# Decoder layer: projections of q, k, v from scaled f16 halves of x, turned by DMA

## The reference

```python
qkv = x @ Wqkv                      # 512 -> 3 x 512
q, k = rmsnorm(q, q_norm_w), rmsnorm(k, k_norm_w)        # over all 512, eps 1e-6
q, k = rope(q), rope(k)             # 16 heads of 32
o = softmax(mask(q k^T / sqrt(32))) v ; x = layernorm(x + o @ Wo)
# cross attention over features: 8 heads of 16 TOKENS each, 512 x 512 scores
qk = einsum('bdm,bdn->bmn', x_heads, ctx_heads) / 4
x = layernorm(x + einsum('bmn,bcn->bcm', softmax(qk), ctx_heads))
# fp8 (e4m3) quantise and dequantise of x and of the weight, blocks of 128
x = layernorm(x + qdq(x) @ qdq(W).T)
```

## Time and profile before

| | us |
|---|---|
| median of 3 runs | 2799.9 (2793.93 to 2802.55) |
| profiled execution, its own time | 2798.56 |
| its span in the trace | 2796.8 |
| TensorE busy | 2586.9 (92%) |
| VectorE busy | 2252.9 (81%) |
| ScalarE busy | 2030.6 (73%) |
| GpSimd busy | 1535.7 (55%) |

### The profile page before, as it was taken

How to read it: one execution, slowest core, us unless ns; L and a number is a source line. 1 busy time by engine, 2 the same in 40 slices (tenths; PEclk the granted TensorE clock), 3 DMA queues, 4 the chain that set the end, 5 groups by cost and what they waited for, 6 DMA issues and landing times.

```text
span 2796.8 us, 65074 instructions
## 1 busy us (share of the span) xinstructions
PE 2586.9 (92%) x19088; PEld 1156.4 (41%) x19088; DVE 2252.9 (81%) x3405; ACT 2030.6 (73%) x2945; POOL 1535.7 (55%) x2393
## 2 busy tenths in 40 slices
PE   0679999999999999999999999999999999999774
PEld 0444444444444444444444444444444444444211
DVE  6247888888888888888888888888888888888751
ACT  0235777887778778887888777877887788777653
POOL 1243556655665556655665566655665566556422
PEclk9779999999999999999999999999999999999866
DMA  2133344434443344434343444334443444344211
GB/s 88 38 82 96 93 115 100 118 96 113 109 111 100 106 118 101 110 97 120 99 117 95 114 106 114 100 105 118 102 109 96 121 99 115 98 115 98 84 37 30
DMA packets 534121, 278.46 MB, mean 100 GB/s; under 512 B 401057, under 2 KB 483105, under 8 KB 534049
## 3 DMA queue, kind: packets, MB, share of 16 engines
q1 hardware_dynamic: 534048, 277.56, 38.4%
HBM read 108.09 MB, written 85.46 MB: 69 GB/s over the span
## 4 chain that ended last, share of the span: by engine, by line
PE 79%; DVE 5%; POOL 5%; ACT 4%; issue 4%; DMA 4%; SPq 0%; ACTq 0%; DVEq 0%; POOLq 0%
PE bank L912 27%; PE pv L1042 15%; PE mx L1015 9%; PE st L1029 9%; PE bank L1051 6%; ACT pp L601 3%; PE bank L979 2%; PE bank L961 2%; DMA xdT<-xd 2%; PE bank L948 2%; PE bank L905 2%; PE bank L951 2%; PE bank L982 2%; DVE nm L761 1%; POOL yq L561 1%
## 5 line engine op out<-in xcount | busy, mean ns | idle before, releaser
L761 DVE TENSOR_REDUCE nm<-mx 128x2 f32<-128x1024 f32 x1024 | 1252.3, 1223 | 265.7 <-PE mx L1015 245.5
L601 ACT ACTIVATE pp<-st,esc 128x1024 f32<-128x1024 f32 x1024 | 1139.7, 1113 | 321.5 <-PE st L1029 259.7
L1042 PE MATMUL pv<-pp,vT 128*32 128x512 f32 x4096 | 550.4, 622 | 0.4 <-ACT pp L601 0.2
L1029 PE MATMUL st<-qp,kp 50*128 50x512 f16 x2048 | 402.8, 390 | 36.2 <-ACT pp L601 34.5
L1015 PE MATMUL mx<-kp,qp 48*128 48x512 f16 x2048 | 401.8, 389 | 28.1 <-DVE nm L761 26.6
L912 PE MATMUL bank<-w_h,xT_h 128*128 128x512 f32 x768 | 349.9, 456 | 4.8 <-DVE xT_l L807 4.7
L912 PE MATMUL bank<-w_l,xT_h 128*128 128x512 f32 x768 | 308.1, 401 | 0.0
L912 PE MATMUL bank<-w_h,xT_l 128*128 128x512 f32 x768 | 305.8, 398 | 0.0
L1015 PEld LDWEIGHTS mx<-kp,qp 48*128 48x128 f16 x2048 | 99.3, 93 | 373.6 <-DVE nm L761 189.9
L912 PEld LDWEIGHTS bank<-w_h,xT_h 128*128 128x128 f32 x768 | 146.6, 191 | 169.8 <-issue 135.7
L528 POOL TENSOR_SCALAR_AFFINE_SELECT p<-p 128x512 f32<-128x512 f32 x256 | 162.9, 636 | 95.1 <-ACT p L644 95.0
(11 more groups left out here) (138 smaller groups left out, 4648.9 us busy)
## 6 DMA issues: line engine op xcount, KB each, us to landing
qp<-q_rows SPq DMA_DIRECT2D x256, 96.0 KB, 2.5
kp<-k_rows SPq DMA_DIRECT2D x256, 96.0 KB, 2.3
xb<-x SPq DMA_DIRECT2D x64, 256.0 KB, 2.6
x_rows<-x SPq DMA_DIRECT2D x64, 256.0 KB, 2.1
q_rows<-qpl SPq DMA_DIRECT2D x64, 256.0 KB, 2.8
cx<-ctx SPq DMA_DIRECT2D x64, 256.0 KB, 2.8
k_rows<-kpl SPq DMA_DIRECT2D x64, 256.0 KB, 2.8
x<-x_rows SPq DMA_DIRECT2D x64, 256.0 KB, 2.8
```

What stands on the lines that cost most here:

```text
L601: a.activation(pp[:, unit % 2, 2 * l:2 * (l + 1), :], st[:], ACT.Exp, scale=esc[b.i][:])\
L761: v.tensor_reduce(cols, mx[:], AX.X, ALU.max, negate=True).then_inc(mx_free, 1)
L1029: last = t.matmul(st[:, q, :], kp[b.i][rows, p, i * P:(i + 1) * P], qp[b.i][rows, p, :], start=True, stop=True)
L1042: last = t.matmul(pv[32 * j:32 * j + 2 * XD, :], vT[b.i][:, i, GROUPS * j + g, :], pp[:, unit % 2, j, :], start=(i == 0), stop=(i == KC - 1))
```

## The change

- Weights `w_h`, `w_l` are f16 halves of Wqkv times a power of two, found in the set-up from the sum of squares. High halves are made by ScalarE, low ones by VectorE; the feed-forward weight takes its scale from its sum of squares too, and the round trip of its maximum through memory is gone. Each quantised block takes its own maximum in the loop over blocks.
- x is no longer transposed by TensorE. ScalarE squares it (`x_square`), TensorE sums over partitions (`x_sum`, two one-column products, the second adds a tiny constant), VectorE makes the scale (`x_exp`), ScalarE and GpSimd the scaled f16 halves (`x_high`, `x_scale`, `x_low`), and SyncE turns them (`turn_x`) into `xsT`. The projections use the helper `split`, which the feed-forward product now uses too.
- q and k keep the scale through the rms (the epsilon is scaled along, `xeps`), v is scaled back when it is copied out (`vinv`).
- `xb` has one buffer; the residual rows are loaded a second time, into `xr` (`ld_xr`).
- `pp` has four units in place of two.
- `ctx_sum` gets the tiny constant too. `junkd` has one buffer per layer norm.
- The five tables of steps and `BANK` are new. The tables of SyncE and TensorE are shown.

```diff
-        w_h, w_l = sb("w_h", [P, KC, 3 * D], F32R), sb("w_l", [P, KC, 3 * D], F32R)
+        w_h, w_l = sb("w_h", [P, KC, 3 * D], F16), sb("w_l", [P, KC, 3 * D], F16)
...
-        xb = [sb(f"xb{i}", [P, D]) for i in range(2)]
-        cx, cxs = sb("cx", [P, D]), sb("cxs", [P, D])
-        xT_h, xT_l = sb("xT_h", [P, D], F32R), sb("xT_l", [P, D], F32R)
+        xb, xr = sb("xb", [P, D]), sb("xr", [P, D])
+        cx, cxs, xf = sb("cx", [P, D]), sb("cxs", [P, D]), sb("xf", [P, D])
+        xs, xsT = sb("xs", [P, 2, D], F16), sb("xsT", [P, 2 * KC, P], F16)
...
+        pp = sb("pp", [P, PB, GH, D])
...
+            ld_kp:1@5 st_qpl:0@4 ld_qp:1@5 turn_xd:0@8 turn_x:0@1 ld_x2r:0@7 ld_qp:0@4 ld_x:0@0
+            st_out:0@8 st_sh1:0@2 st_kpl:0@4 ld_sh1:0@2 ld_kp:0@4 st_sh2:0@5 st_x2:0@3 ld_xr:0@2
+            ld_sh2:0@5 turn_parts:0@1 ld_cx:0@3 turn_parts:1@1""")
...
+            cross_scores_T:10@6 proj_k:2@1 proj_k:3@1 cross_scores:14@5 proj_v:0@1 proj_v:1@1
+            self_scores_T:0@2 cross_scores_T:11@6 cross_scores:15@5 proj_v:2@1 proj_v:3@1
+            self_scores_T:1@2 cross_scores_T:12@6 cross_scores:0@4 cross_pv:3@6 self_pv:0@2
+            self_scores_T:2@2 cross_scores_T:13@6 self_pv:1@2 cross_scores:1@4 self_scores_T:3@2
+            cross_pv:4@6 self_pv:2@2 cross_scores:2@4 cross_scores_T:14@6 self_pv:3@2 cross_pv:5@6
+            cross_scores_T:15@6 cross_scores:3@4 cross_pv:6@6 context_T:0@4 cross_scores_T:0@5
+            x_sum:0@0 cross_pv:7@6 cross_scores:4@4 cross_scores_T:1@5 proj_o:0@2 proj_o:1@2
+            cross_scores:5@4 cross_scores_T:2@5 proj_o:2@2 proj_o:3@2 cross_scores:6@4
+            cross_scores_T:3@5 self_scores:0@1 self_scores:1@1 ctx_sum:0@3 cross_pv:0@5
+            cross_scores:7@4 cross_scores_T:4@5 self_scores:2@1 ffn:0@7 ffn:1@7 cross_scores_T:5@5
+            cross_scores:8@4 ffn:2@7 ffn:3@7 cross_scores_T:6@5 cross_scores:9@4 proj_q:0@0
+            self_scores:3@1 cross_scores_T:7@5 cross_scores:10@4 proj_q:1@0 proj_q:2@0
+            cross_scores_T:8@5 cross_scores:11@4 proj_q:3@0 proj_k:0@0 proj_k:1@0 cross_scores:12@4
+            cross_scores_T:9@5 cross_pv:1@5 cross_pv:2@5 cross_scores:13@4""")
...
             def ld_x(b, _):
-                sp.wait_ge(*freed("wo", b, -2))
-                sp.sem_inc(passed_sp, 1)
-                sp.dma_start(xb[b.i][:], x[b.idx()]).then_inc(d_x[b.i], 16)
+                sp.wait_ge(s_xsl, b.n(1, 0))
+                sp.sem_inc(passed_sp, 1)
+                sp.dma_start(xb[:], x[b.idx()]).then_inc(d_x, 16)
+
+            def ld_xr(b, _):
+                sp.wait_ge(*freed("wo", b, -1))
+                sp.sem_inc(passed_sp, 1)
+                sp.dma_start(xr[:], x[b.idx()]).then_inc(d_xr, 16)
...
+            def turn_x(b, _):
+                sp.wait_ge(s_xsl, b.n(1, 1))
+                sp.sem_inc(passed_sp, 1)
+                sp.wait_ge(*full("v", b, -1))
+                sp.sem_inc(passed_sp, 1)
+                sp.dma_start_transpose(xsT[:], xs[:].rearrange("p a d -> p (a d)")).then_inc(d_xsT, 16)
...
+            def x_scale(b, _):
+                pool.wait_ge(s_sx, b.n(1, 1))
+                pool.sem_inc(passed_pool, 1)
+                g_.tensor_scalar(xf[:], xb[:], sx[b.i][:], 1.0, ALU.mult, ALU.mult).then_inc(s_xf, 1)
+                g_.tensor_scalar(xeps[b.i][:], sx[b.i][:], sx[b.i][:], weps[:], ALU.mult, ALU.mult).then_inc(s_xeps, 1)
+
+            def x_low(b, _):
+                pool.wait_ge(s_xf, b.n(1, 1))
+                pool.sem_inc(passed_pool, 1)
+                pool.wait_ge(s_xsh, b.n(1, 1))
+                g_.tensor_tensor(xs[:, 1, :], xf[:], xs[:, 0, :], ALU.subtract).then_inc(s_xsl, 1)
...
+            for c in range(KC):
+                act.wait_ge(d_setup[c], 16)
+                a.activation((qp[0], qp[1], qs, ks)[c][:].bitcast(BF16).rearrange("p a d -> p (a d)")[:, 0:3 * D],
+                             pp[:, c].rearrange("p a d -> p (a d)")[:, 0:3 * D], ACT.Square,
+                             accum_out=wss[:, 0, c:c + 1]).then_inc(u_wss, 1)
+            act.wait_ge(d_wffn, 16 * KC)
+            for c in range(KC):
+                a.activation((junk, junkc, junkd[0], junkx)[c][:], wf_rows[c][:], ACT.Square, accum_out=wss[:, 1, c:c + 1]).then_inc(u_wss, 1)
+            act.wait_ge(u_wsc, 1)
+            for n in range(2 * KC):
+                hi = (w_h, wo_h)[n // KC]
+                src = pp[:, n % PB].rearrange("p a d -> p (a d)")[:, 0:hi.shape[2]]
+                act.wait_ge(d_setup[n % PB], 16 * (n // PB + 1))
+                a.activation(hi[:, n % KC, :], src, ACT.Copy, scale=(wsc[:, 0:1], 1.0)[n // KC]).then_inc(u_high, 1)
...
-                act.wait_ge(pv_unit, b.n(UNITS, unit - 1))
-                a.activation(pp[:, unit % 2, 2 * l:2 * (l + 1), :], st[:], ACT.Exp, scale=esc[b.i][:])\
+                act.wait_ge(pv_unit, b.n(UNITS, unit + 1 - PB))
+                a.activation(pp[:, unit % PB, 2 * l:2 * (l + 1), :], st[:], ACT.Exp, scale=esc[b.i][:])\
                  .then_inc(st_free, 1)
...
-            def xT_high(b, _):
-                act.wait_ge(*full("v", b, -1))
-                act.wait_ge(*full("xT", b))
-                a.activation(xT_h[:], at("xT")[:], ACT.Copy).then_inc(s_xTh, 1)
+            def x_square(b, _):
+                act.wait_ge(d_x, b.n(16, 16))
+                act.wait_ge(*full("xt", b, -1))
+                act.wait_ge(s_xss, b.n(1, 0))
+                a.activation(junkx[:], xb[:], ACT.Square, accum_out=xss[:]).then_inc(s_xss, 1)
+
+            def x_high(b, _):
+                act.wait_ge(s_sx, b.n(1, 1))
+                act.wait_ge(d_xsT, b.n(16, 0))
+                a.activation(xs[:, 0, :], xb[:], ACT.Copy, scale=sx[b.i][:]).then_inc(s_xsh, 1)
...
-            def xT_low(b, _):
-                dve.wait_ge(s_xTh, b.n(1, 1))
-                v.tensor_tensor(xT_l[:], at("xT")[:], xT_h[:].bitcast(F32), ALU.subtract)\
-                 .then_inc(bank_free[BANK["xT"]], 1)
+            def x_exp(b, _):
+
+                dve.wait_ge(*full("xt", b))
+                v.tensor_scalar(xbits[:], at("xt")[:, 0:1].bitcast(I32), -0.5, SCALE_TOP, ALU.mult, ALU.add)\
+                 .then_inc(bank_free[BANK["xt"]], 1)
+                dve.wait_ge(*freed("xt", b))
+                dve.wait_ge(s_xsl, b.n(1, -1))
+                dve.wait_ge(s_xeps, b.n(1, -1))
+                v.tensor_scalar(sx[b.i][:].bitcast(I32), xbits[:], EXP_BITS, None, ALU.bitwise_and).then_inc(s_sx, 1)
+                dve.wait_ge(s_sx, b.n(1, 1))
+                dve.wait_ge(*freed("v", b, -2))
+                v.tensor_scalar(vinv[b.i][:].bitcast(I32), sx[b.i][:].bitcast(I32), -1.0, wtop[:], ALU.mult, ALU.add)\
+                 .then_inc(s_vinv, 1)
...
+            def split(name, lin, wh, wl, cols, part):
+
+                for i, (lo, w) in enumerate(((0, wh), (0, wl), (1, wh))):
+                    last = t.matmul(at(name)[:], lin[:, KC * lo + part, :], w[:, part, cols], start=(part == 0 and i == 0),
+                                    stop=(part == KC - 1 and i == 2))
+                if part == KC - 1:
+                    last.then_inc(bank_full[BANK[name]], 1)
+
+            def x_sum(b, _):
+                pe.wait_ge(s_xss, b.n(1, 1))
+                pe.wait_ge(*before("xt", b))
+                t.matmul(at("xt")[:, 0:1], ones[:], xss[:], start=True, stop=False)
+                t.matmul(at("xt")[:, 0:1], ones[:], tiny[:], start=False, stop=True).then_inc(bank_full[BANK["xt"]], 1)
 
             def proj_q(b, part):
                 if part == 0:
-                    for point in last_of(
-                            freed("xT", b),
-                            before("q", b),
-                    ):
-                        pe.wait_ge(*point)
-                linear("q", xT_h, xT_l, w_h, w_l, slice(0, D), part)
+                    pe.wait_ge(d_xsT, b.n(16, 16))
+                    pe.wait_ge(*before("q", b))
+                split("q", xsT, w_h, w_l, slice(0, D), part)
...
-                t.matmul(at("ct")[:, 0:1], ones[:], css[:], start=True, stop=True).then_inc(bank_full[BANK["ct"]], 1)
+                t.matmul(at("ct")[:, 0:1], ones[:], css[:], start=True, stop=False)
+                t.matmul(at("ct")[:, 0:1], ones[:], tiny[:], start=False, stop=True).then_inc(bank_full[BANK["ct"]], 1)
```

More of the change, by code:

```diff
@@ L729, in _ @@
[L729 to L733 removed]
+            dve.wait_ge(u_wss, 2 * KC)
@@ new lines, in _ @@
+            v.tensor_reduce(wsum[:], wss[:], AX.X, ALU.add).then_inc(u_wsum, 1)
+            dve.wait_ge(u_wtot, 1)
+            step(v.tensor_scalar(wbits[:], mx[:, 0, 0:2].bitcast(I32), -0.5, SCALE_TOP, ALU.mult, ALU.add))
+            step(v.tensor_scalar(wsc[:].bitcast(I32), wbits[:], EXP_BITS, None, ALU.bitwise_and))
+            v.tensor_scalar(wtop[:], wsc[:, 0:1].bitcast(I32), -1.0, float(3 * ONE_BITS * 2 ** 23), ALU.mult, ALU.add)
+            v.tensor_scalar(weps[:], wsc[:, 0:1], wsc[:, 0:1], RMS_EPS, ALU.mult, ALU.mult)
@@ new lines, in _ @@
```

(24 more changed lines are left out.)

173 lines of the change are left out of this document (70 added, 103 removed).

## The result

The kernel after takes 2735.82 us (median of 4 runs, 2733.5 to 2741.84), the one before 2801.23 (4 runs, 2793.93 to 2806.02). The ratio is 0.9777 [0.976, 0.9795]. The profiled execution has a span of 2740.1 us (before 2796.8): 56.7 us less.

The account below looks back on a forecast made before the run. TensorE's own stream was taken to bound the steady loop. From 2798.6 us, -66 for the loop and +3 for set-up and filling gave 2735.6, plus 1.3 for the median: 2737 us, chance 0.68, range 2695 to 2784.

Parts of the forecast that it names:

- the loop: Steady part: -1.1 us a turn (between -1.8 and -0.1), over 60 of the 64 batches -66 us.
- set-up with filling: Before the steady loop: blocks' maxima +3, first batch +4, three filling slots -4; total +3 us, between -8 and +14.
- Projections: 36 projection matmuls a turn: f32r to f16, 0.233 to 0.217 us each, 0.20 to 0.10 per group; gain 1.4 us.
- spacing by columns alone: Rival: f32r projection matmuls lose only their group openings, gain 0.5 us a turn, 2773 us; chance 0.02.
- Sums against transposes: TensorE's turn: three more one-column products +0.75 us, x's four transposes gone -0.56; +0.2 us (between -0.2 and +0.6).
- Order of the steps: Cross-score runs on TensorE: 18 in place of 17, +0.1 us a turn; groups with the probabilities unchanged.
- Stalls left unchanged: TensorE's stalls, under 1% of the turn, kept in the sum; bounds -0.5 us to +0.8 us from VectorE's thinner slack.
- Wait for the turned x: Before the first q product: x's transpose has 1.9 us of slack, so the wait was costed at nothing.
- the slower rival: Turn of x is late, TensorE waits before q0 each turn; 2 us of waiting gives 2857 us; chance 0.09.
- Draining: Last slots, without projections: zero, but +-10 us because their order is new.
- more than summed: Rival: the new order also shortens stalls, filling and draining, 2675 us; chance 0.06.
- stalls by VectorE and ScalarE: Rival: their lost slack turns into TensorE stalls, gain 0 to 0.5 us a turn, 2773 to 2803; chance 0.15.

Follow-up runs that it names:

- e2: Kernel before, only the projection operands (halves of x and Wqkv) made f16 without a scale, order and transposes kept: 2738.23 us, ratio 0.977.
- e3: Changed kernel with its 36 projection matmuls a turn reading f32r tiles (the split output weight), waits and order kept: 2796.28 us, ratio 0.9981 to the kernel before.
- e1: Changed kernel with the transpose of the quantised rows issued before the second load of q rows in SyncE's queue: 2685.22 us, ratio 0.959 to the kernel before.
- e6: Kernel of e1 with the transpose of x moved behind the load of the residual rows in SyncE's queue: 3059.36 us, ratio 1.0923.
- e5: Kernel before with x loaded a second time for the residual add, nothing else: 2785.25 us, ratio 0.9952.
- e4: Kernel of e2 with four units of probabilities (`pp`) in place of two, in the old order: 2739.31 us, ratio 0.9777 to the kernel before.

## Why the prediction was right, and where it was wrong

The forecast of 2737 us met 2735.82, but two of its terms were off by about 29 us each, in opposite directions: the loop (said -66, measured -37) and set-up with filling (said +3, measured -25.5). That they cancelled is luck. Of the signs that it named, the spacing, the weight loads and the missing wait in front of q came; the turn is 38.87 us, not 38.3, and VectorE is busy for 86.5% of the stretch, not 89. The 39.36 us that it took for the old turn is the shorter of the two in the loop's body; their mean is 39.55.

- **Projections: right.** Said -1.4 us a turn, measured -1.44. The two parts, 0.233 to 0.217 per matmul and 0.20 to 0.10 per group, hold in the rows: a group of 6 and one of 9 take 1.60 and 2.30 us before, 1.40 and 2.05 after. The runs bear out their sum: e2 changes the form in 7 groups (1.28 by these prices, measured 1.21), e3 undoes it in 6 (1.18, measured 1.14). The weight loads are 97 ns, as the feed-forward's were the earlier trace rows. The rival of spacing by columns alone is refuted by the same two runs. The gap of 216 ns for 512 columns in the Trainium skill (TensorE: Matmul & The Clock Gate, Back-to-back issue gap) fits the f16 rows here and not the f32r ones.
- **Sums against transposes: right.** Said +0.75 - 0.56, measured +0.77 - 0.64.
- **Order of the steps: too dear.** Said +0.1 for one more run of cross steps. The probabilities times values cost 0.29 less and the transposed self scores 0.13 less, where nothing was credited. Without the new stall the turn's difference is -1.69, not -1.1. The rows name most of it. The prediction took the groups of 8 products with the probabilities as unchanged, without a look at what follows them. In the new order two of the groups stand right before the self attention's own products with values, and such a group takes 0.88 us to the next start, where the others take 0.97 to 1.00. That is 0.23 of the 0.29:

```profile
1370.43 1.06 PE L1112 MATMUL pv<-pp,vT 128*32 128x512 f32 x8
1371.31 0.40 PE L1048 MATMUL bank<-p,va 128*32 128x128 f32 x8
```

  The 0.13 is about the size of the old wait for the exponentials (8.3 us in 49 turns), which stood behind such a self score and is gone. No run changes either of the two alone.
- **Stalls left unchanged: the step that failed.** Stalls per turn went from 0.2 to 1.0 us, that is to the upper bound given (+0.8). But that bound was argued from VectorE's thinner slack, and e1 refutes this for the new order: VectorE at 89% stalls nobody. (In the old order it does, by 0.25 us a turn in e2.) The place was passed over. The step on the turned x priced GpSimd's chain and TensorE's cover for x, and called the transpose of the quantised rows only what stands ahead of it; it didn't walk down SyncE's new list and add the issue times ahead of that transpose (6.6 us for a transpose and six plain DMAs, from 1380.30 to 1386.90 above). In place of -66 us the loop gave -37 over 55 turns; at -1.1 a turn these 55 would have given -60, the other 5 of the 60 lie in draining here.
- **Wait for the turned x: right.** Costed at nothing with 1.9 us of slack, and no wait shows. From issue to use a late transpose takes 3.5 us (e6, 1373.81 to 1377.35). In the turn of the kernel after the transpose is issued at 1388.47 and q starts at 1394.08, so 2.1 are left; in the turn of e1 it is 1362.00 and 1366.69, so 1.2. e6 shows the slower rival's mechanism beyond that, and that at a wait of 4.8 us the price is higher than the wait, since the clock falls too. No run has the wait of 2 us that the rival priced.
- **Set-up: half right; filling: wrong.** The loop was to start where it did; it starts at 67.01, 3.9 us earlier, since the copies and subtractions were done at 35.5, not at 41. The blocks' own maxima cost what was said, 2.9 us. The rows of the kernel after, VectorE's first maximum of a block, then the start of the loop on ScalarE and TensorE, against the earlier trace rows:

```profile
35.48 0.68 DVE L789 TENSOR_REDUCE amax<-x 128x4 f32<-128x512 f32 x1
```

```profile
67.01 0.63 ACT L658 ACTIVATE junkx<-xb 128x512 bf16<-128x512 f32 x1 [32.18 <-DVE amax L805]
```

```profile
75.15 0.61 PE L983 MATMUL bank<-w_h,xsT 128*128 128x512 f16 x1 [6.33 <-DMA xsT<-xs]
```

The first chain of x takes 8.1 us (said: about 8), so the first projection is at 75.15, 0.3 later than before. Between there and batch 0's feed-forward the kernel gains 25.8 us, where 4 were credited. The prediction looked at filling only for removed copies and held the second load of x to be free; it didn't see that the load of batch 2's x had been waiting for batch 0's residual add. e5 puts that at 10.4, the types give 2.1 (e2) and the four units 3.5 (e4). If these add up, 9.5 are left for the turned x and the new order together. But in the new order the types are worth more: with f32r operands put back (e3), batch 0's feed-forward comes at 304.38, 6.8 us later than in the kernel after, and then 5 are left. Each figure is of one profile, and the kernel after and e1, which hardly differ in filling, are 1.9 us apart there (297.57, 299.44). This was not separated further.
- **Draining:** said 0 +-10, measured +5.6; no run looks for its cause.

The rival "more than summed" was right on filling alone: stalls and draining got longer, not shorter. That of stalls by VectorE and ScalarE named the right kind of loss and the wrong engine.

## What to carry to other kernels

When an order is written anew, walk down every queue, that of the DMA issuer first: add the issue times of the entries ahead of each transfer whose user has little slack, and compare when its data is ready with when it is issued. Data that was ready at 1385.47 and a transfer that was issued at 1386.90 were worth 50 us here. Keep set-up, filling, loop and draining as separate sums, since a right total can hide two wrong ones; and read in the filling slots what each load waits for, because a buffer that never binds in the loop can bind there.

## What the hardware showed beside this

- A DMA transpose holds SyncE's queue for 1.25 us (one of 128 x 1024 f16) or longer (of q and k, 128 x 2048 f16): in the kernel after q's 1.9 us and k's 2.8 in the median, k's between 2.1 and 3.1, where k's took 1.9 before. A plain transfer holds it for 0.3 to 0.6 in the median. Three transposes and six plain ones, back to back from 1380.30 to 1389.70, are a quarter of a turn.
- After 4.8 us without a matmul TensorE ran for some 4.5 us at the lower level of its clock (granted 0.54 in the mean, e6); this cost a further 1.8 us per turn of 44.4. After 1.0 us of waiting it did not (granted 1.00 in the kernel after).
- f32r and f16 differ at the same number of columns by about 0.017 us per matmul and 0.09 to 0.10 us per group (groups of 6 and 9: 1.60 and 2.30 us against 1.40 and 2.05). Both directions of the edit (e2, e3) give their sum.
- The same group of 8 products takes 0.88 or 1.00 us to the next start, depending on what kind of product follows (kernel after, above).
